# Convolution taps of a state-space stage: shifted copies made through a DRAM scratch in place of copies inside SBUF

## The chip, the cores and the metric

The kernel is one program on one core of a Trainium2 chip. The metric is the device time of that program in microseconds (us), median of several executions. TensorE is PE in the rows of the profile (its weight loads PEld), VectorE is DVE, ScalarE is ACT, GpSimd is POOL. SyncE (SP, its DMA queue SPq) computes nothing here: it waits on semaphores and issues DMAs.

## The reference

Two transformer-like layers run on `x` of 32 batches x 128 steps x 128 channels. The change lies in the first layer's second stage, a Mamba-2 block, which begins with a causal depthwise convolution over 16 steps on 384 channels (256 of `x`, 64 of `B`, 64 of `C`):

```python
zxbcdt = x @ W_in
z = zxbcdt[..., :D_INNER]
xBC = zxbcdt[..., D_INNER:D_INNER + CONV_DIM]
dt = jax.nn.softplus(zxbcdt[..., -NHEADS:] + dt_bias)
kernel = conv_w.T[:, None, :]
xBC = jax.lax.conv_general_dilated(xBC, kernel, window_strides=(1,), padding=[(D_CONV - 1, 0)], ...,
                                   feature_group_count=CONV_DIM) + conv_b
xBC = jax.nn.silu(xBC)
```

A scan over the 128 steps, a gated norm and two projections follow. Before this stage stands a GRU over time, behind it an attention block (cond2), a mixture of experts, and then the second layer.

## The kernel before, in words

Each engine has its own instruction stream, written out by Python generators: `weave` takes one turn of each lane in rotation, so the order on an engine is fixed when the program is built, and semaphores alone decide when an instruction starts. In the stage of the change PE, ACT and DVE each weave four lanes: the convolution (`conv_*`), the step sizes (`mdt_*`), and two workers of the scan (`mamba_*`, worker 0 and worker 1), which start some turns later. SP has only the convolution's lane (`conv_sp`), after its loads and before the loads of the next stage.

The convolution is done in 24 pieces. Piece `n` is one group of 128 channels (`n % 3`) for one unit of four batches (`n // 3`), so its tile is 128 partitions x 512. Its steps:

- **In-projection.** PE makes it into PSUM bank 6 (`inputs` in `conv_pe`; `B<-G,win`), two pieces ahead of the taps. ACT copies it into `XP[n % 4]`, a tile of 4 batches x 144 steps of which the first 16 are zero (`inputs` in `conv_act`, semaphore `conv.x`; shown in the trace as `work<-B`, and `spare<-B` for every fourth piece, since `XP[3]` lies in the area `spare`).
- **Shifted copies.** Twelve of the sixteen taps are done on PE as matmuls that contract over 128 partitions = 32 channels x 4 shifts. For that, `XR[n % 2]` (in `spare`, 130 steps for each of 16 rows) holds in partitions 32g to 32g+31 the tile shifted by 3g steps, and along the free axis the four groups `j` of 32 channels. `conv_sp` fills it by 16 DMAs (4 shifts x 4 channel groups) of 32 partitions x 4 batches x 130 words, 65 KB each, when `conv.x` of the piece and the taps of piece n-2 (which used the same buffer) are done.
- **Taps on PE.** In three turns, `m` = 0, 1, 2, each with four matmuls for the four channel groups (`B<-spare,work` in the trace, two records for each matmul, so x8 for one turn and x24 for a piece). They wait for the semaphore `conv.r0` or `conv.r1` of the 16 DMAs, and for `conv.b` of the piece before, which frees the only PSUM bank of the taps (bank 7).
- **The rest.** ACT takes the bank out with the bias (`work<-B,cb`, `conv.b`), DVE adds the last four taps from `XP` (`conv.acc`), ACT makes a tanh, DVE the silu (`conv.silu`).

ACT's order matters here. In the turns of piece n it does the bias of n-1, the tanh of n-2, and then the copy `XP` of piece n+2. After the first piece it also computes the step sizes (`mdt`) and the decays of both workers (`catt<-tri,catt`, eight for each worker and batch), which PE's cumulative sums (`catt,low`) wait for.

Of the kernel before, what the change touches and what calls it, by code (L numbers as in the profile page):

```python
# [6 lines left out]
F32 = mybir.dt.float32  # L7
# [9 lines left out]
class Signals:  # L17
# [15 lines left out]
    def inc(self, name, *key, by=1):  # L33

        self.value[name] = self.value.get(name, 0) + by
        if self.counting:
            self.place[(name, *key)] = self.value[name]
        return self.sem(name), by

    def dma(self, name, *key):  # L40
        return self.inc(name, *key, by=16)

    def at(self, name, *key):

        if self.counting:
            return self.sem(name), 1
        return self.sem(name), self.place[(name, *key)]
# [54 lines left out]
def act(e, out, in_, func, bias=0.0, scale=1.0):  # L102
    return e.activation(out, in_, func, bias=bias, scale=scale)  # L103
# [35 lines left out]
NT = 12  # L139
# [24 lines left out]
class Kernel:  # L164
# [26 lines left out]
    def sb(self, name, shape, dt=F32):  # L191
        return self.ctx.enter_context(self.nc.sbuf_tensor(name, shape, dt))
# [399 lines left out]
    def lay_mamba(self):  # L592
        sb = self.sb
        self.win = sb("win", [128, 648])
        self.wout = sb("wout", [128, 2, 128])
        self.wnl = sb("wnl", [128, 128])
        self.bnl = sb("bnl", [128, 1])
        self.nw = sb("nw", [128, 2])
        self.cw = sb("cw", [128, 3, 16])
        self.cb = sb("cb", [128, 3])  # L600
        self.dtb = sb("dtb", [128, 8])
        self.alog = sb("alog", [128, 8])
        self.dcol = sb("dcol", [128, 2])
        self.dg = sb("dg", [128, 2, 128])
        self.h0 = sb("h0", [128, 2, 64])
        self.h0T = sb("h0T", [64, 256])
        self.cwp = sb("cwp", [128, 12, NT // 4])
        self.id32 = sb("id32", [128, 32])
        self.tap = self.area([self.work, 74 * 256 - 96 * NT], [128, 3 * NT, 32])
        w = [self.spare, 0]  # L610
        self.XR = [self.area(w, [128, 16, 127 + NT // 4]) for _ in range(2)]
        w = [self.work, 0]
        ar = lambda *s, dt=F32: self.area(w, list(s), dt)
        self.cvb = [ar(128, 3, 512) for _ in range(4)]
        self.c0b = [ar(128, 512) for _ in range(3)]
        self.XP = [ar(128, 4, 144) for _ in range(3)]
        self.XP.append(self.area([self.spare, 5120 - 576], [128, 4, 144]))
        self.cth = [ar(128, 512) for _ in range(2)]
        c = [self.catt, 6144]
        self.adt, self.dth, self.ec, self.q1, self.q2, self.q3 = (self.area(c, [128, NB, 8]) for _ in range(6))  # L620
        self.mw = []
        for wk in range(2):
            wc = [self.catt, wk * 3072]
            m = {"E": [self.area(wc, [128, 8, 128]) for _ in range(2)], "z": [self.area(wc, [128, 256]) for _ in range(2)]}
            m |= {"xdt": ar(128, 256), "cbm": ar(128, 128), "y4": ar(128, 4, 256), "sq": self.area(c, [128, 256]),
                  "ss": ar(128, 4), "yT": ar(128, 2, 512), "tm": ar(128, 512)}
            self.mw.append(m)
# [172 lines left out]
    def conv_act(self, e):  # L800

        at, inc = self.at, self.inc
        BI, BT = self.bank[6], self.bank[7]

        def taps_out(n):
            u, c = n // 3, n % 3
            e.wait_ge(*at("conv.taps", n))
            if u >= 4 and c == 0:
                e.wait_ge(*at(f"mw{u % 2}.pe", "y", (u - 4) // 2 * 4 + 3))
            act(e, self.cvb[u % 4][:, c, :], BT[:], ACT.Identity, bias=self.cb[:, c:c + 1]).then_inc(*inc("conv.b", n))  # L810

        def tanh(n):
            e.wait_ge(*at("conv.acc", n))
            if n >= 2:
                e.wait_ge(*at("conv.silu", n - 2))
            act(e, self.cth[n % 2], self.cvb[n // 3 % 4][:, n % 3, :], ACT.Tanh, scale=0.5).then_inc(*inc("conv.th", n))
        e.wait_ge(*at("conv.pad"))

        def inputs(n):
            e.wait_ge(*at("conv.in", n))  # L820
            if n >= 4:
                e.wait_ge(*at("conv.acc", n - 4))
                e.wait_ge(*at(f"conv.r{n % 2}", n - 4))
            act(e, self.XP[n % 4][:, :, 16:144], BI[:].rearrange("p (b t) -> p b t", b=4), ACT.Copy).then_inc(
                *inc("conv.x", n))
        inputs(0)
        yield
        inputs(1)
        yield
        n = 0  # L830
        for u in range(8):
            for c in range(3):
                if n:
                    taps_out(n - 1)
                if n >= 2:
                    tanh(n - 2)
                yield
                if n < 22:
                    inputs(n + 2)
                for _ in range(3):  # L840
                    yield
                n += 1
            yield
        taps_out(n - 1)
        tanh(n - 2)
        for _ in range(4):
            yield
        tanh(n - 1)
# [37 lines left out]

    def conv_sp(self, e):

        for n in range(24):
            e.wait_ge(*self.at("conv.x", n))  # L890
            if n >= 2:
                e.wait_ge(*self.at("conv.taps", n - 2))
            else:
                e.wait_ge(*self.at("conv.pad"))
            for g in range(4):
                for j in range(4):
                    e.dma_start(self.XR[n % 2][32 * g:32 * g + 32, 4 * j:4 * j + 4, :],  # L897
                                self.XP[n % 4][32 * j:32 * j + 32, :, 1 + NT // 4 * g:128 + NT // 4 * (g + 1)]).then_inc(*self.dma(f"conv.r{n % 2}", n))

    def conv_pool(self, e):  # L900
        e.wait_ge(*self.at("xt", 7))
# [1799 lines left out]
```

## Time and profile before

| | |
|---|---|
| Median of 3 runs | 2227.7 us (2224.23 to 2228.19) |
| The profiled execution's own time | 2227.43 us |
| Its span in the profile | 2225.7 us |
| PE busy, of the span | 1960.3 us (88%) |
| DVE busy | 1593.2 us (72%) |
| ACT busy | 1006.9 us (45%) |
| DMA issues of the convolution | 384 (288 `spare<-work`, 96 `spare<-spare`) of 65.0 KB |
| The stage of the change | from 234 us to about 600 us of the span |

The span is the time from the first to the last instruction that the profiler shows; the execution's own time is 1.7 us longer. Times in rows are counted from the span's start. A row of the timeline gives start and duration, the instruction, how many are merged into it, and in brackets how long the engine had been idle and what ended that. The taps of piece n begin on PE at 249.27 (n = 0), 259.83, 270.84, 280.53, 290.87, 302.21 (n = 5), and so on up to 546.23 (n = 23).

### The profile page before, as it was taken

The numbers are of one execution on the slowest core, as the hardware profiler recorded it, in microseconds if no ns is written. First come the engines' busy times: TensorE is split into PE (matmuls) and PEld (weight loads), VectorE is DVE, ScalarE is ACT, GpSimd is POOL, SyncE is SP. The second block draws the span as 40 slices with busy tenths as digits, with TensorE's granted clock in tenths as the row PEclk, the third lists the DMA queues.
The fourth block names the chain that finished last, engine by engine and source line by source line (L and its number), as shares of the span: only waits on it lengthen the run. The fifth ranks groups of instructions, "written<-read, shape, count | busy, mean of one in ns | idle before, by whom it ended". The sixth has DMA issues, their size and how long they took to land.

```text
span 2225.7 us, 63875 instructions
## 1 busy us (share of the span) xinstructions
PE 1960.3 (88%) x26197; PEld 1227.9 (55%) x26273; DVE 1593.2 (72%) x3661; ACT 1006.9 (45%) x2843; POOL 466.7 (21%) x816
## 2 busy tenths in 40 slices
PE   8989688888778989887899999967999789999998
PEld 5555233333353434434577767655666456677776
DVE  3444557777647787876988888726989578888887
ACT  3333347666622222122555555433554445555554
POOL 2221000000002343434012122254331111112100
PEclk9999789999969899997999999978999999999999
DMA  3000344332000000002211111016552211111111
GB/s 66 4 4 4 74 99 87 71 85 53 30 24 0 1 1 1 1 1 62 76 45 43 45 43 45 25 38 127 110 100 54 67 40 45 45 45 45 42 57 37
DMA packets 133228, 102.42 MB, mean 46 GB/s; under 512 B 23532, under 2 KB 114244, under 8 KB 131364
## 3 DMA queue, kind: packets, MB, share of 16 engines
q1 hardware_dynamic: 129352, 96.04, 17.8%
q8 instruction: 206, 3.38, 0.6%
q10 hardware_dynamic: 3584, 2.30, 0.3%
q14 instruction: 86, 0.70, 0.1%
HBM read 60.24 MB, written 11.82 MB: 32 GB/s over the span
## 4 chain that ended last, share of the span: by engine, by line
PE 47%; DVE 24%; ACT 12%; issue 9%; SPq 3%; DMA 2%; ACTq 1%; POOL 1%; another core or an unknown queue 0%; DVEq 0%; POOLq 0%
PE B L85 46%; DVE work L2251 4%; ACT catt L103 4%; DVE work L107 4%; DVE hr L2215 3%; DVE work L2259 3%; SPq L897 2%; ACT hr L103 2%; ACT ltc L103 2%; ACT work L103 2%; DVE work L1627 1%; DVE gzh L107 1%; ACT ghh L103 1%; ACTq L2538 1%; DVE lth L107 1%
## 5 line engine op out<-in xcount | busy, mean ns | idle before, releaser
L85 PE MATMUL B<-gr,wres 128*128 128x512 f32 x1248 | 352.9, 411 | 15.8 <-DVE work L2259 9.4
L103 ACT ACTIVATE work<-B 128x512 f32<-128x512 f32 (+6 forms) x462 | 236.3, 528 | 143.8 <-PE B L85 99.4
L2301 POOL COPY G<-lh 128x32 f32<-128x32 f32 x256 | 148.3, 579 | 679.9 <-DVE lh L107 679.9
L85 PEld LDWEIGHTS B<-gr,wres 128*128 128x128 f32 x1248 | 214.1, 189 | 82.6 <-DVE work L2259 26.8
L103 ACT ACTIVATE hr<-work 128x512 fp32r<-128x512 f32 x272 | 172.9, 636 | 147.8 <-DVE work L2259 77.8
L2215 DVE TENSOR_TENSOR hr<-work,hr 128x512 fp32r<-128x512 f32 x272 | 186.5, 686 | 8.1 <-ACT hr L103 6.6
L2251 DVE TENSOR_TENSOR work<-work 128x512 f32<-128x512 f32 x256 | 178.6, 698 | 14.7 <-ACT work L103 7.2
L85 PE MATMUL B<-hr,wres 128*128 128x512 f32 x624 | 178.0, 394 | 1.0 <-DVE hr L2215 1.0
L103 ACT ACTIVATE lth<-B 128x96 f32<-128x96 f32 (+1 forms) x512 | 86.7, 222 | 185.9 <-PE B L85 185.8
L85 PEld LDWEIGHTS B<-lh,lw 128*32 128x32 f32 x8128 | 88.5, 112 | 112.8 <-issue 58.6
L85 PE MATMUL B<-lh,lw 128*32 128x32 f32 x8128 | 116.7, 199 | 25.1 <-DVE lh L107 24.3
L107 DVE SCALAR_TENSOR_TENSOR work<-B,ckc,work 128x512 f32<-128x512 f32 x160 | 116.6, 741 | 27.6 <-ACT work L103 18.3
L85 PE MATMUL B<-work 128*128 128x128 bf16 (+2 forms) x1120 | 122.7, 232 | 15.5 <-DMA work<-work 6.2
L85 PEld LDWEIGHTS B<-hr,wres 128*128 128x128 f32 x624 | 117.2, 188 | 28.0 <-DVE hr L2215 1.9
L1627 DVE TENSOR_TENSOR work<-B,work 128x512 f32<-128x512 f32 x160 | 106.6, 680 | 34.9 <-remote 33.9
L103 ACT ACTIVATE catt<-catt 128x512 f32<-128x512 f32 (+2 forms) x142 | 81.7, 590 | 109.3 <-DVE catt L2551 89.8
L1664 POOL TENSOR_TENSOR work<-work 128x512 f32<-128x512 f32 x64 | 82.1, 1283 | 212.5 <-DVE work L1627 118.5
L107 DVE SCALAR_TENSOR_TENSOR lh<-lth,ltc 128x32 f32<-128x32 f32 x256 | 49.4, 193 | 106.3 <-ACT ltc L103 106.3
L85 PE MATMUL B<-gr,hr 128*128 128x512 f32 x384 | 114.1, 435 | 9.5 <-DVE gr L1566 7.0
L85 PE MATMUL B<-X,lw 128*128 128x128 f32 x512 | 121.5, 322 | 0.0
L85 PEld LDWEIGHTS B<-work 128*128 128x128 bf16 (+2 forms) x1120 | 86.0, 108 | 63.4 <-issue 26.7
L85 PE MATMUL B<-gr,wr 128*128 128x512 f32 x384 | 109.6, 420 | 4.0 <-DVE work L2259 2.2
(270 smaller groups left out, 3850.2 us busy)
## 6 DMA issues: line engine op xcount, KB each, us to landing
work<-wdr SPq DMA_DIRECT2D x128, 256.0 KB, 3.1
spare<-work SPq DMA_DIRECT2D x288, 65.0 KB
scr<-catt SPq DMA_DIRECT2D x144, 64.0 KB, 2.8
spare<-spare SPq DMA_DIRECT2D x96, 65.0 KB
work<-scr SPq DMA_DIRECT2D x16, 384.0 KB
work<-scr SPq DMA_DIRECT2D x16, 192.0 KB
catt<-in_L_ffn_ew SPq DMA_DIRECT2D x24, 128.0 KB, 2.4
work<-scr SPq DMA_DIRECT2D x16, 128.0 KB
```

What stands on the lines that cost most here:

```text
L85: return e.matmul(out, lhsT, rhs, start=start, stop=stop, skip_group_check=True)
L103: return e.activation(out, in_, func, bias=bias, scale=scale)
L107: return e.scalar_tensor_tensor(out=out, in0=a, scalar=s, in1=b, op0=op0, op1=op1)
L897: e.dma_start(self.XR[n % 2][32 * g:32 * g + 32, 4 * j:4 * j + 4, :], self.XP[n % 4][32 * j:32 * j + 32, :, 1 + NT // 4 * g:128 + NT // 4 ...
L1627: e.tensor_tensor(four(pr[n % 6]), four(B[:]), KP[:, c, :, j:j + 128], ALU.mult).then_inc(*inc(dve, "v", i, c, j))
L1664: e.tensor_tensor(av, u0, u1, ALU.add).then_inc(*inc(f"cd{wk}.pool", i, c))
L2215: e.tensor_tensor(hr[1][:], self.hh[j % 4], hr[0][:].bitcast(F32), ALU.subtract).then_inc(*self.inc("m.dve", "h", li, j))
L2251: e.tensor_tensor(src, self.sg[i], self.Wb[n % 4], ALU.mult).then_inc(*inc("m.dve", "pu", li, k))
L2259: h = stt(e, self.hh[m], U, 0.5, src, ALU.mult, ALU.mult) if li else e.tensor_tensor(self.hh[m], U, src, ALU.mult)
L2301: e.tensor_copy(self.G[:, :, t], self.lh[:, t % 4, :]).then_inc(*inc("l.pool", "h", li, t))
L2538: e.dma_start(self.aQ[u % 4][48 + q:49 + q, :, :], self.anT[16 * q:16 * q + 16, :]).then_inc(*self.dma("at.max", u))
```

## The change

Each piece now goes out to a scratch in DRAM (`xdr`, four buffers of 32 x 16 x 144 words) by one DMA of 288 KB, and comes back by four DMAs, one for each shift `g`, of 32 partitions x 16 rows x 130 words (260 KB). The transposition of the channel groups (128 partitions x 4 batches into 32 partitions x 16) is done by the outgoing DMA's address pattern on the DRAM side. The outgoing DMA of piece n+1 is issued ahead of the four incoming ones of piece n. Two new semaphores, `conv.w0` and `conv.w1`, count the outgoing DMAs; ACT's copy into `XP` of piece n waits for the outgoing DMA of n-4 in place of the 16 copies of n-4. Everything else of the program is the same.

```diff
         self.XR = [self.area(w, [128, 16, 127 + NT // 4]) for _ in range(2)]
+        self.xdr = [self.nc.dram_tensor(f"xdr{i}", [32, 16, 144], F32, kind="Internal").ap() for i in range(4)]
...
-                e.wait_ge(*at(f"conv.r{n % 2}", n - 4))
+                e.wait_ge(*at(f"conv.w{n % 2}", n - 4))
...
     def conv_sp(self, e):
 
+        at, dma = self.at, self.dma
+
+        def write(n):
+            e.wait_ge(*at("conv.x", n))
+            if n >= 4:
+                e.wait_ge(*at(f"conv.r{n % 2}", n - 4))
+            e.dma_start(self.xdr[n % 4].rearrange("p (j b) t -> j p (b t)", j=4), self.XP[n % 4][:]).then_inc(
+                *dma(f"conv.w{n % 2}", n))
+        e.wait_ge(*at("conv.pad"))
+        write(0)
         for n in range(24):
-            e.wait_ge(*self.at("conv.x", n))
+            if n < 23:
+                write(n + 1)
+            e.wait_ge(*at(f"conv.w{n % 2}", n))
             if n >= 2:
-                e.wait_ge(*self.at("conv.taps", n - 2))
-            else:
-                e.wait_ge(*self.at("conv.pad"))
+                e.wait_ge(*at("conv.taps", n - 2))
             for g in range(4):
-                for j in range(4):
-                    e.dma_start(self.XR[n % 2][32 * g:32 * g + 32, 4 * j:4 * j + 4, :],
-                                self.XP[n % 4][32 * j:32 * j + 32, :, 1 + NT // 4 * g:128 + NT // 4 * (g + 1)]).then_inc(*self.dma(f"conv.r{n % 2}", n))
+                e.dma_start(self.XR[n % 2][32 * g:32 * g + 32, :, :],
+                            self.xdr[n % 4][:, :, 1 + NT // 4 * g:128 + NT // 4 * (g + 1)]).then_inc(*dma(f"conv.r{n % 2}", n))
```

Only SP's stream changes its order. This is SP at the start of the convolution before the change, pieces 1 to 3 (`spare` on the left is `XR`, on the right `XP`):

```order
L897 DMA spare<-work 32x4x130 [waits s_conv.pad,s_conv.x]
L897 DMA spare<-work 32x4x130 x15
L897 DMA spare<-work 32x4x130 [waits s_conv.taps,s_conv.x]
L897 DMA spare<-work 32x4x130 x15
L897 DMA spare<-spare 32x4x130 [waits s_conv.taps,s_conv.x]
L897 DMA spare<-spare 32x4x130 x15
```

And this is SP at the same place with the change, up to the first incoming DMA of piece 3 (`xdr0` to `xdr3` are the four scratches, in DRAM):

```order
L896 DMA xdr0<-work 4x32x576 [waits s_conv.x,s_conv.pad]
L896 DMA xdr1<-work 4x32x576 [waits s_conv.x]
L907 DMA spare<-xdr0 32x16x130 [waits s_conv.w0]
L907 DMA spare<-xdr0 32x16x130 x3
L896 DMA xdr2<-work 4x32x576 [waits s_conv.x]
L907 DMA spare<-xdr1 32x16x130 [waits s_conv.w1]
L907 DMA spare<-xdr1 32x16x130 x3
L896 DMA xdr3<-spare 4x32x576 [waits s_conv.x]
L907 DMA spare<-xdr2 32x16x130 [waits s_conv.taps,s_conv.w0]
L907 DMA spare<-xdr2 32x16x130 x3
L896 DMA xdr0<-work 4x32x576 [waits s_conv.r0,s_conv.x]
L907 DMA spare<-xdr3 32x16x130 [waits s_conv.taps,s_conv.w1]
```

Sixteen DMAs per piece have become five, the shape of the outgoing one begins with 4 where all the others begin with 32, and ahead of the incoming DMAs of a piece there now stands a wait for `conv.x` of the next piece.

## Rows read from the trace of the kernel before

**Rows 1.** View of waits, 228 to 600 us: who waited for whom, total us, times, longest.

```profile
PE B L85 <- DMA spare<-work: 19.1, 5, 7.0
PE B L85 <- DMA spare<-spare: 5.1, 1, 5.1
```

**Rows 2.** Stretch, us, busy of PE, PEld, DVE, ACT, POOL; PE's clock, DMA share, GB/s.

```profile
236.00:302.00 66.00, 41.85 (x203) 12.77 (x200) 33.47 (x82) 21.55 (x52) 0.00 (x0) 0.72 0.45 98
```

**Rows 3.** Timeline of SP's queue: the convolution's first 48 DMA issues.

```profile
236.01 32.44 SPq L897 DMA_DIRECT2D spare<-work  x48
```

**Rows 4.** The DMA issues of the convolution: duration of one, min/median/max ns.

```profile
L897 SPq DMA_DIRECT2D spare<-work x288: 585/601/2046, 236.0 to 524.1; - x144
```

**Rows 5.** Timeline of PE: the taps (spare,work) and the first sums (catt,low).

```profile
249.27 5.24 PE L85 MATMUL B<-spare,work 128*32 128x512 f32 x24 [7.05 <-DMA spare<-work]
259.83 1.93 PE L85 MATMUL B<-spare,work 128*32 128x512 f32 x8 [4.11 <-DMA spare<-work]
261.70 5.08 PE L85 MATMUL B<-catt,low 128*128 128x512 f32 x8
266.70 1.94 PE L85 MATMUL B<-spare,work 128*32 128x512 f32 x16
270.84 1.93 PE L85 MATMUL B<-spare,work 128*32 128x512 f32 x16 [0.29 <-ACT work L103]
280.53 4.97 PE L85 MATMUL B<-spare,work 128*32 128x512 f32 x24 [5.07 <-DMA spare<-spare]
290.87 3.64 PE L85 MATMUL B<-spare,work 128*32 128x512 f32 x16 [4.32 <-DMA spare<-work]
302.21 1.94 PE L85 MATMUL B<-spare,work 128*32 128x512 f32 x8 [2.82 <-DMA spare<-work]
...
324.43 1.07 PE L85 MATMUL B<-spare,work 128*32 128x512 f32 x8
335.15 1.07 PE L85 MATMUL B<-spare,work 128*32 128x512 f32 x8 [0.82 <-DMA spare<-work]
...
363.46 1.07 PE L85 MATMUL B<-spare,work 128*32 128x512 f32 x8
```

**Rows 6.** Timeline of ACT: decays, and copies into XP (pieces 0,1,3-6,8,11).

```profile
235.38 0.60 ACT L103 ACTIVATE work<-B 128x512 f32<-128x512 f32 x1 [2.20 <-PE B L85]
239.50 0.60 ACT L103 ACTIVATE work<-B 128x512 f32<-128x512 f32 x1 [1.03 <-PE B L85]
256.14 4.77 ACT L103 ACTIVATE catt<-tri,catt 128x128 f32<-128x128 f32 x16
260.81 0.57 ACT L103 ACTIVATE spare<-B 128x512 f32<-128x512 f32 x1
271.81 0.59 ACT L103 ACTIVATE work<-B 128x512 f32<-128x512 f32 x1
276.95 0.58 ACT L103 ACTIVATE work<-B 128x512 f32<-128x512 f32 x1
286.68 0.59 ACT L103 ACTIVATE work<-B 128x512 f32<-128x512 f32 x1
313.89 0.60 ACT L103 ACTIVATE work<-B 128x512 f32<-128x512 f32 x1
...
352.07 0.59 ACT L103 ACTIVATE spare<-B 128x512 f32<-128x512 f32 x1
```

**Rows 7.** DMA, 235.9 to 240.9 us: busy tenths in slices of 0.125 us.

```profile
DMA  0000000000004982627840178510000000497303
```

**Rows 8.** DMA, 256.8 to 260 us: packets of the copies inside SBUF.

```profile
DMA packets 720, 0.33 MB, mean 104 GB/s; under 512 B 80, under 2 KB 720, under 8 KB 720
```

**Rows 9.** DMA, 9 to 13 us: loads of 512 B runs from DRAM, all engines busy.

```profile
DMA packets 2510, 1.18 MB, mean 296 GB/s; under 512 B 216, under 2 KB 2510, under 8 KB 2510
```

**Rows 10.** DMA, 608 to 612.5 us: loads, nearly half of the packets of 4 KB.

```profile
DMA packets 831, 1.69 MB, mean 376 GB/s; under 512 B 35, under 2 KB 476, under 8 KB 830
```

**Rows 11.** DMA, 1045.8 to 1047.2 us: one DMA out to DRAM, 8 rows of 2 KB.

```profile
DMA packets 16, 0.02 MB, mean 12 GB/s; under 512 B 8, under 2 KB 8, under 8 KB 16
```

## The prediction

> **What bounds the kernel now.** I read three views, in this order. The view of waits over the stage says what PE waits for: 24.2 us of its idle time end when a copy into `XR` lands, six waits in all [rows 1]. The stretches say where: from 236 to 302 us PE is busy for 41.9 of 66.0 us, at a clock of 0.72, with DVE and ACT busy for 33.5 and 21.6 us, so that no engine is the bound there, and neither are the DMA engines at a share of 0.45 [rows 2]. The timeline of SP then shows what is: 48 issues without a gap take 32.44 us, 0.676 us each [rows 3, 4], or 10.8 us for the 16 of a piece, and the taps of pieces 1 to 5 start 10.6, 11.0, 9.7, 10.3 and 11.3 us after each other [rows 5]. The waits of PE in it are 7.05, 4.11, 5.07, 4.32 and 2.82 us. From piece 6 on both workers of the scan fill PE, and only 0.82 us more is lost, before piece 8 [rows 5]. So all that the change can win lies between 249 and 335 us, and is at most about 24 us.
>
> **What the change does, part by part.** *Issues.* Five for 16 at 0.6 us each [rows 4], some 3.2 us of SP per piece: SP is no bound any more. *What is late next* is the latency from ACT's copy to a filled `XR`, because it now has two DMAs in series, and because SP issues the incoming four of piece n only behind the outgoing one of piece n+1. They cannot start before ACT has made the copy of piece n+1. I call R the time from the end of that copy to the moment when PE can use `XR` of piece n.
>
> R has four terms. (a) From issue to first packets: the first issue is at 236.01 and the busy tenths begin in the 13th slice, at 237.4, so 1.4 us [rows 3, 7]. (b) The outgoing 295 KB. A DMA with 8 outermost rows of 2 KB shows 8 small packets beside 8 large ones [rows 11], while the five issues with 32 outermost partitions show 80, so 16 each [rows 8]. I take the small packets as one closing packet for each DMA engine used: a leading 8 ran on 8 engines, and the outgoing DMA leads with 4. Large packets run at 376 GB/s over 16 engines [rows 10], 23.5 per engine, so four engines need 295/94 = 3.1 us, where 16 would need 0.8. (c) The incoming DMAs are queued behind it on these four engines. Each engine has 128 packets of 520 B and 4 small ones. A packet takes 25.5 ns in the loads (4 us x 16 / 2510) [rows 9] and about 34 ns in the copies into 32 partitions (0.45 x 16 x 460 B / 98 GB/s, with 0.33 MB / 720 = 460 B) [rows 2, 8]: 3.4 to 4.5 us. I take the middle, 3.9. (d) Landing: the 32nd issue, the last of piece 1, ended near 236.01 + 32 x 0.676 = 257.6 and began 0.6 before; PE went on at 259.83, 2.8 us after its begin. Less 1.4 for (a) and 0.6 of packets (five slices), 0.8 us are left [rows 3, 5, 7]. R = 1.4 + 3.1 + 3.9 + 0.8 = 9.2 us. The 0.65 us of the outgoing issue and 2.6 us of the four incoming ones lie beside (b).
>
> By the Trainium skill (DMA: Bandwidth & Descriptors, Rules for kernel authors) "an outermost dim of size c < 16" confines a whole DMA to at most c engines; the 8 closing packets agree with it, and it speaks against this change, whose outgoing pattern puts the four channel groups outermost. By this rule (b) is 3.1 us, as taken; without it, 0.8.
>
> *The walk.* Pieces 0 and 1 first. The copies of 0 and 1 end at 235.98 and 240.10 [rows 6]. Outgoing 0 has landed at 236.0 + 1.4 + 3.1 + 0.8 = 241.3. Outgoing 1 holds its four engines until 244.6, incoming 0 follows on them until 248.5: PE can start at 249.3, as before (249.27). On these engines outgoing 2 takes until 251.6 and incoming 1 until 255.5, so `XR` of piece 1 is ready at 256.3. PE comes to it at 259.83 - 4.11 = 255.7, and starts 3.5 us earlier than before. Next come the sums of both workers. They need the decays, which ACT ends at 258.5 (first eight) and 260.9 [rows 6] and which do not move. The first worker's sums run from 258.5, the second's end at 260.9 + 2.5 = 263.4, where both ended at 266.78. So the rest of the taps of piece 1 is 3.1 us earlier.
>
> From here each piece has two bounds, and the later one counts: PE's arrival (its start before, less its wait, less the lead won so far), and the copy of the next piece + R.
> - Piece 2: copy 3 ends at 261.4 and stands behind the decays, so it does not move; + 9.2 = 270.6, against 270.84. Lead 0.2.
> - Piece 3: copy 4 ended at 272.4, and follows the taps of piece 1, so 269.3 + 9.2 = 278.5, against 280.53. Lead 2.0.
> - Piece 4: copy 5, 277.53 - 0.2 = 277.3, gives 286.5; PE arrives at 286.55 - 2.0 = 284.5. Against 290.87, lead 4.4.
> - Piece 5: copy 6, 287.27 - 2.0 = 285.3, gives 294.5; PE arrives at 299.39 - 4.4 = 295.0. Against 302.21, lead 7.2.
> - Piece 8: the last 0.8 us of waiting. Lead 8.0. The starts of all of these are in [rows 5, 6].
>
> In the later pieces the distance from a copy to the taps of the piece before it must be over 9.2 us. The smallest is 324.43 - 314.49 = 9.9, the next is 363.46 - 352.66 = 10.8 [rows 5, 6]; of the rest one more has 10.8 and six have 11.1 to 11.9. So there R is hidden, if with little to spare. What covers the double latency is the scan's work on PE.
>
> *At no cost:* ACT's copy waits for the outgoing DMA of n-4 in place of the copies of n-4, both long done; the wait of an outgoing DMA for the incoming ones of n-4 likewise; the 33 MB through DRAM meet no other transfer of the stage. Behind the wait for the copy of n+1 SP has only the incoming DMAs of n, counted in R. After the convolution SP's next loads wait for the scan's end. A shorter wait could also raise PE's clock from 0.72 [rows 2]; I book nothing for it.
>
> The sum is made against the profiled execution's own 2227.4 us, 0.3 below the median of the runs: 2227.4 - 8.0 = 2219.4 us.
>
> **Bounds.** The unknown prices are (b) and (c). With (b) at 3.1 and (c) at 3.4 and landing half a microsecond shorter, R = 8.2, and the same walk gives a lead of 11 us. With R = 10 it gives 6.5. If the outgoing packets take half as long again (4.6 us), R = 10.7, and 4 us are left. Reads of DRAM into 32 partitions are not in the trace; their two neighbours are the ends of (c).
>
> The copies inside SBUF run at 98/0.45 = 218 GB/s of all engines, the loads into 128 partitions at 296 [rows 2, 9]. By the Trainium skill (SBUF — State Buffer, Door 1: The DMA port swizzle) 32 partitions reach 8 of 16 ports and end near 218 GB/s; the trace agrees. By this the incoming DMAs would take 4.9 us where all engines run together, R would be about 10, and the time 2221.
>
> **The rivals.**
> 1. *The outgoing DMA runs on 16 engines.* Then (b) is 0.8, R = 6.9, piece 0 starts 2.3 us earlier, the walk gives leads of 4.8, 6.6, 10.9 and 13.7 us at pieces 2 to 5 and 14.5 in the end: 2213 us. For it: the source leads with 128 partitions, and the transfer is large. Against it: the 8 closing packets [rows 11].
> 2. *R is 10.2 to 11.5*, since outgoing packets into DRAM are slow, or the issue of the incoming ones stalls behind the four busy engines (single issues took up to 2.05 us [rows 4]). The waits then stay on the early pieces, with another cause: a lead of 6 down to 0, at R = 10.9 some 3.5 us: 2224 us.
> 3. *Slower.* With R = 12 the copy of the next piece decides everywhere, in the full part of the stage too. The walk then gives leads of -2.6, -0.8, -1.2 and +1.6 us at pieces 2 to 5. Piece 7 loses 2.1 us (12 against 9.9), the two with 10.8 lose 1.2 each, and the six others 0.1 to 0.9 each, 3.1 together: 7.6 lost, 1.6 + 0.8 won, so 2233 us. It decides from R = 11.5 on. For it: two DMAs in series on four engines, and a wait of SP for the piece after. Against it: it needs 2.8 us more than rows show anywhere.
>
> **How the numbers follow.** The forecast (lead 6 to 11 us) has 0.52, rival 1 (over 11) 0.16, rival 2 (lead under 6) 0.22, rival 3 0.10. The likeliest gives 2219.4 us. The range reaches down to 2212, which takes in rival 1 at its price, and up to 2225.5, which takes in nearly all of rival 2. A measurement of this kernel can tell 0.2%, 4.5 us, from no change. Forecast and rival 1 are all faster by more, and a third of rival 2: 0.75. The rest of rival 2 and a little of rival 3 lie within: 0.17. Slower: 0.08.
>
> **What the profile would show.** The outgoing DMAs should show four small packets each, and bursts on a quarter of the engines. PE's first taps should start within a microsecond of 249.3, its later waits for the incoming DMAs should be near 0.6, 2.9, 3.3 and 2.0 us at pieces 1 to 4, none at 5, and 9 us should lie between the end of ACT's copy of a piece and the taps of the piece before it, at pieces 2 to 4. From piece 6 on the timeline should be the old one, 7 to 8 us earlier, and so the rest of the kernel. I am wrong if PE's first taps start near 247 (16 engines), if waits on DMA appear at pieces 7 and 10 (R over 10), or if the lead won by 302 us is given back before 600.

## The result, and the profile after

The changed kernel takes 2238.2 us, the median of 20 runs, against 2225.5 us of as many runs of the kernel before: a ratio of 1.0060, with a 95% interval of 1.0048 to 1.0072. It is about 13 us slower, where 2219.4 was forecast and 2225.5 was the upper end of the range. That is a change of 0.6%, small but clear of the noise. Rival 3 of the prediction came true in kind (2233 us, chance 0.10). The profiled execution took 2237.95 us, its span 2236.2; before they were 2227.43 and 2225.7. So 10.5 of the 13 us are to be found in the two traces.

PE's waits from 228 to 610 us, us in total, times, the longest:

```profile
PE B L85 <- DMA spare<-xdr: 35.7, 12, 11.2
```

It was 24.2 us in six waits [rows 1]. SP issues little now and sleeps long: the wait ahead of the outgoing DMA (L896) holds it for 180 us, half of the stage. The view of SP's waits, from 228 to 600 us:

```profile
SPq L896 <- ACT work L103: 124.0, 15, 14.4
SPq L896 <- ACT spare L103: 56.3, 6, 11.2
```

The taps of PE (start, duration, then in brackets PE's wait before them), for pieces 0 to 4 and then where a wait on `XR` is left:

```profile
253.49 4.83 PE L85 MATMUL B<-spare,work 128*32 128x512 f32 x24 [11.19 <-DMA spare<-xdr]
260.19 1.07 PE L85 MATMUL B<-spare,work 128*32 128x512 f32 x8 [0.65 <-DMA spare<-xdr]
...
277.23 3.64 PE L85 MATMUL B<-spare,work 128*32 128x512 f32 x16 [6.68 <-DMA spare<-xdr]
284.80 2.79 PE L85 MATMUL B<-spare,work 128*32 128x512 f32 x24 [0.99 <-DMA spare<-xdr]
296.78 3.64 PE L85 MATMUL B<-spare,work 128*32 128x512 f32 x16 [8.14 <-DMA spare<-xdr]
...
317.89 1.08 PE L85 MATMUL B<-spare,work 128*32 128x512 f32 x8 [0.25 <-DMA spare<-xdr]
328.22 1.07 PE L85 MATMUL B<-spare,work 128*32 128x512 f32 x8 [1.08 <-DMA spare<-xdr]
337.96 1.07 PE L85 MATMUL B<-spare,work 128*32 128x512 f32 x8
...
370.09 1.07 PE L85 MATMUL B<-spare,work 128*32 128x512 f32 x8 [1.15 <-DMA spare<-xdr]
412.76 1.07 PE L85 MATMUL B<-spare,work 128*32 128x512 f32 x8 [1.22 <-DMA spare<-xdr]
...
549.12 1.07 PE L85 MATMUL B<-spare,work 128*32 128x512 f32 x8 [2.04 <-DMA spare<-xdr]
```

Against [rows 5], pieces 0 to 4 start 4.2, 0.4, 6.4, 4.3 and 5.9 us later, and piece 8 (337.96) 2.8 us later. Before, PE waited for `XR` nowhere after piece 8. Now it does at pieces 10, 13, 16, 19 and 22.

R can be read off against the copies of ACT (pieces 3, 4 and 5):

```profile
264.63 0.57 ACT L103 ACTIVATE spare<-B 128x512 f32<-128x512 f32 x1
272.32 0.58 ACT L103 ACTIVATE work<-B 128x512 f32<-128x512 f32 x1
283.93 0.59 ACT L103 ACTIVATE work<-B 128x512 f32<-128x512 f32 x1
```

The copy of piece 3 ends at 265.20 and PE starts on piece 2 at 277.23: R = 12.0. The next two give 284.80 - 272.90 = 11.9 and 296.78 - 284.52 = 12.3; at pieces 6, 7, 10, 13, 16 and 19 it is 11.7 to 12.1. It was taken as 9.2. It is longer at piece 22 (12.9), and at pieces 0 and 1 (13.3 and 17.3), whose outgoing DMAs queue behind others. SP's queue, which [rows 3] showed as 48 issues in a row, is now:

```profile
236.11 4.61 SPq L896 DMA_DIRECT2D xdr<-work  x2
242.85 2.69 SPq L907 DMA_DIRECT2D spare<-xdr  x4
...
265.23 0.56 SPq L896 DMA_DIRECT2D xdr<-spare  x1
266.30 3.54 SPq L907 DMA_DIRECT2D spare<-xdr  x4
```

Outgoing 0 is issued at 236.11, and the first incoming DMA, which waits for it, at 242.85: 6.7 us for 295 KB (the 288 KB above in units of 1024 bytes). From 237.3 to 242.3 us it runs all but alone (slices of 0.125 us):

```profile
DMA  1243904900200013221331112222222222242119
GB/s 55 55 55 37 150 0 18 37 0 0 18 0 0 18 55 74 74 74 55 74 55 55 74 55 111 111 92 111 92 111 111 92 111 92 111 111 74 55 55 74
```

It begins well, then hardly a packet starts for a microsecond (single packets of 2304 B take up to 1.0 us, against 0.09 in the median), then it goes at 55 to 74 GB/s, and only in its last part at 92 to 111. These are 23 to 28 GB/s for each of four engines, the rate that was taken for the whole. Over its packets, some 5.2 us, it moves 57 GB/s, 14 from each. What makes the start slow was not tried. In e2 below, where the same DMA stands behind incoming ones on its engines, it has no such start, and its packets take 3.3 to 3.9 us at pieces 1 to 8, nearer to the 3.1 of the prediction.

That it is four engines is shown by the small packets from 228 to 600 us:

```profile
DMA packets 53891, 33.13 MB, mean 89 GB/s; under 512 B 1632, under 2 KB 50784, under 8 KB 53856
```

1632 = 96 x 16 for the incoming DMAs + 24 x 4 for the outgoing ones. The rule of the Trainium skill that the prediction weighed (DMA: Bandwidth & Descriptors, Rules for kernel authors: an outermost size below 16 bounds the number of engines) agrees.

*R, taken apart.* The trace also holds the time at which each engine reports its share of a DMA to the semaphore. Outgoing 3, issued at 265.23, is reported by its four engines at 271.12, 271.26, 272.71 and 272.79. The last report of the incoming DMAs of piece 2 comes at 277.19, and PE starts at 277.23. So 7.6 us pass until the outgoing DMA has landed, and 4.4 more until the incoming ones have. At the other pieces of early and full part at which PE waits (3, 4, 6, 7, 10, 13, 16, 19) the two parts are 7.6 to 8.7 and 3.3 to 4.6 us, in the median 7.7 and 4.0. The view of the DMA engines from 266 to 278 us (slices of 0.3 us) shows why the second part is short:

```profile
DMA  0150527696677989999999997432239997366997
```

From 267.7 the other twelve engines already carry their shares of the incoming DMAs, and by 273.8 they are done. From there to 275 only the four late engines still work, at 0.2 to 0.3 of 16.

The incoming issues (duration of one, min/median/max ns) became longer too:

```profile
L907 SPq DMA_DIRECT2D spare<-xdr x96: 538/984/2073, 242.9 to 546.8; - x96
```

An incoming issue takes 0.98 us in the median, where issues had taken 0.60 [rows 4]. This is not in the chain: the last of piece 2 ends at 269.83, before the outgoing DMA has landed at 272.79, and it is so at every early piece.

*Where the 10.5 us arise.* The last taps start at 568.92, before at 553.86: 15.1 us later. Of these 2.8 were there at piece 8, and 12.3 come in the full part, in which six pieces take 89.0 us in place of 85.3. The stretches (columns as in [rows 2]), first of before, then of after:

```profile
345.00:430.30 85.30, 74.14 (x826) 32.59 (x826) 62.52 (x109) 58.12 (x141) 3.55 (x2) 0.98 0.36 78
```

```profile
349.00:438.00 89.00, 75.66 (x828) 32.55 (x824) 62.64 (x109) 58.09 (x140) 3.54 (x2) 0.96 0.42 93
```

Of the 3.7 us, two waits of 1.15 and 1.22 us are idle time, and 1.5 us is busy time of PE for the same work at a clock of 0.96 in place of 0.98. Over the whole full part (335.15 to 553.86 before, 337.96 to 568.92 after) PE is busy for 195.5 us in place of 190.7, so 4.8 of the 12.3 us are busy time, and 6.7 are waits for `XR`. About 4 us are given back later, in the stage after the scan, of before and of after:

```profile
660.10:1032.30 372.20, 324.19 (x1363) 151.66 (x1376) 287.83 (x475) 81.14 (x132) 146.31 (x118) 0.93 0.01 2
```

```profile
674.60:1042.50 367.90, 322.67 (x1382) 148.93 (x1376) 287.71 (x475) 81.11 (x132) 146.28 (x118) 0.94 0.01 2
```

The first stretch begins 14.5 us later and the end lies 10.2 later. PE's busy time accounts for 1.5 of the 4.3 us; the rest is idle time, whose cause was not tried.

### The profile page after: what moved, and what is told of

It is laid out like the page before. It is cut to its first block, busy times and chain, and to the rows that moved or that the text cites. A ratio compares the mean times of both kernels' runs of the same rounds, so it can differ in the third digit from the quotient of the medians.

```text
span 2236.2 us, 63706 instructions
## 1 busy us (share of the span) xinstructions
PE 1966.7 (88%) x26273; PEld 1225.0 (55%) x26273; DVE 1593.4 (71%) x3661; ACT 1006.7 (45%) x2843; POOL 466.0 (21%) x816
## 4 chain that ended last, share of the span: by engine, by line
PE 46%; DVE 24%; ACT 12%; issue 8%; DMA 5%; SPq 2%; ACTq 1%; POOL 1%; DVEq 0%; POOLq 0%
PE B L85 44%; DVE work L2261 5%; DVE work L107 4%; DMA spare<-xdr 3%; ACT catt L103 3%; DVE hr L2225 3%; DVE work L2269 3%; ACT hr L103 2%; ACT work L103 2%; ACT ltc L103 2%; ACTq L2548 1%; DVE gzh L107 1%; ACT ghh L103 1%; SPq L907 1%; DVE work L1637 1%
## 5 line engine op out<-in xcount | busy, mean ns | idle before, releaser
L85 PE MATMUL B<-gr,wres 128*128 128x512 f32 x1248 | 354.5, 412 | 16.5 <-DVE work L2269 10.2
L107 DVE SCALAR_TENSOR_TENSOR work<-B,ckc,work 128x512 f32<-128x512 f32 x160 | 116.6, 741 | 27.0 <-ACT work L103 17.6
L85 PE MATMUL B<-spare,work 128*32 128x512 f32 x576 | 81.8, 657 | 35.7 <-DMA spare<-xdr 35.7
```

The costliest lines, as they stand in the source:

```text
L85: return e.matmul(out, lhsT, rhs, start=start, stop=stop, skip_group_check=True)
L107: return e.scalar_tensor_tensor(out=out, in0=a, scalar=s, in1=b, op0=op0, op1=op1)
```

## The experiments

Two theories of why R is 12: (A) the outgoing DMA holds four engines for long, and the incoming packets and issues queue behind it; (B) the order is to blame, since the incoming DMAs of a piece are issued only behind the outgoing one of the next. Both can be true, and each has its own cure. A third theory, (C) in the texts below, was that the incoming DMAs are slow by themselves. All edits are against the changed kernel except where said. In the table the second number is the kernel before on the same chip, and the ratio is to it, with its 95% interval; the last column is PE's time waiting for `XR` and the number of waits.

| run | time, us | before, us | ratio | waits |
|---|---|---|---|---|
| before | | 2225.5 | | 24.2, 6 |
| the change | 2238.2 | 2225.5 | 1.0060 (1.0048 to 1.0072) | 35.7, 12 |
| e1_out16 | 2219.8 | 2225.4 | 0.9970 (0.9954 to 0.9986) | 21.7, 6 |
| e2_order | 2225.8 | 2225.4 | 1.0000 (0.9986 to 1.0013) | 25.0, 6 |
| e3_both | 2216.8 | 2225.4 | 0.9964 (0.9949 to 0.9979) | 16.2, 5 |
| e4_twice | 2278.1 | 2225.4 | 1.0240 (1.0222 to 1.0257) | 60.4, 14 |
| e5_long_in | 2216.7 | 2224.2 | 0.9964 (0.9950 to 0.9977) | 17.3, 4 |
| e6_both_long | 2209.3 | 2224.2 | 0.9931 (0.9916 to 0.9946) | 12.2, 5 |
| e7_direct_long | 2224.3 | 2224.2 | 1.0008 (0.9995 to 1.0020) | 21.5, 5 |
| e8_in128 | 2200.3 | 2225.2 | 0.9885 (0.9841 to 0.9929) | 9.7, 4 |
| e9_in32 | 2212.6 | 2225.2 | 0.9952 (0.9920 to 0.9984) | 17.6, 5 |
| e10_one_in_before | 2214.8 | 2226.5 | 0.9947 (0.9926 to 0.9968) | 13.7, 4 |
| e11_one_in_behind | 2206.4 | 2226.5 | 0.9904 (0.9876 to 0.9932) | 5.2, 4 |

**e1_out16**: the outgoing copy in four DMAs of 32 partitions each, which run on 16 engines; the order stays.

```diff
-            e.dma_start(self.xdr[n % 4].rearrange("p (j b) t -> j p (b t)", j=4), self.XP[n % 4][:])...
+            for j in range(4):
+                e.dma_start(self.xdr[n % 4][:, 4 * j:4 * j + 4, :], self.XP[n % 4][32 * j:32 * j + 32])...
```

> The outgoing transfer of a piece is four DMAs of 32 partitions (each leads with 32, so 16 engines) in place of one that leads with 4. Nothing else changes. R is the time from the end of ACT's copy of piece n+1 to the first taps of piece n where PE waits for them; it was 11.7 to 12.3 us in the changed kernel. Theory A (four engines carry the outgoing bytes, and incoming packets and their issues are queued behind them): incoming issues fall from a median of 984 ns to about 600, R falls to 8.5 to 9.5 although SP issues three more DMAs (1.9 us), no wait for the incoming DMAs after piece 6, and the time is 5 to 10 us below that of the kernel before. Theory C (the incoming DMAs of 512 runs out of DRAM are slow by themselves): issues stay near 1 us, R stays at 12 or grows by the 1.9 us to 13 to 14, and the time is 12 to 25 us above before.

```profile
263.46 1.71 SPq L897 DMA_DIRECT2D xdr<-spare  x4
265.27 2.55 SPq L908 DMA_DIRECT2D spare<-xdr  x4
...
273.31 3.64 PE L85 MATMUL B<-spare,work 128*32 128x512 f32 x16 [4.53 <-DMA spare<-xdr]
```

R is 273.31 - 263.43 = 9.9 us, 2.1 less than with four engines, if more than the 8.5 to 9.5 expected; the incoming issues are back at 0.627 us in the median, and of the waits at pieces 10 to 22 only 0.33 us is left. This edit alone turns 13 us slower into 6 us faster, so (A) is shown. Outgoing copy 3 lands 3.0 us after its first issue in place of 7.6, yet R falls by 2.1 only. From the first incoming issue to PE it still takes 8.0 us, and the packets of 520 B in it take 5.9: R is not the 6.9 of rival 1. So (C) holds in part as well, if not in the 12 to 25 us that it forecast: once all 16 engines bring the incoming bytes together, they take longer than the four late engines of the changed kernel took for their own shares.

**e2_order**: the outgoing DMA stays on four engines, and `write(n + 1)` stands behind the incoming issues of piece n.

```diff
-            if n < 23:
-                write(n + 1)
             e.wait_ge(*at(f"conv.w{n % 2}", n))
 ...
             for g in range(4):
                 e.dma_start(self.XR[n % 2][32 * g:32 * g + 32, :, :], ...
+            if n < 23:
+                write(n + 1)
```

> The outgoing DMA stays on its four engines, but SP issues the incoming DMAs of piece n before the outgoing one of piece n+1, so they no longer wait for ACT's copy of n+1. Theory B (the place in SP's order is what makes the latency count in the full part of the stage): the five or six waits of about 1.1 us each from piece 6 on are gone, PE's first taps start 2 to 3 us earlier than in the changed kernel (near 250.5), a piece of the early part costs SP one landing of the outgoing DMA (6.7 us) and the four issues (2.6 us), 9.3 to 10.5 in all, so the time is 3 to 8 us below before. If the order does not matter (the latency is the engines' work itself), it stays within 4 us of the changed kernel, 12 us above before.

```profile
274.71 2.57 SPq L905 DMA_DIRECT2D spare<-xdr  x4
277.38 0.55 SPq L896 DMA_DIRECT2D xdr<-work  x1
285.07 2.56 SPq L905 DMA_DIRECT2D spare<-xdr  x4
287.73 0.55 SPq L896 DMA_DIRECT2D xdr<-work  x1
295.55 2.56 SPq L905 DMA_DIRECT2D spare<-xdr  x4
```

Now there is no wait behind piece 8 (0.54 us), since in the full part a copy lies long ahead of its use. In the early part each piece costs SP a whole round: 2.6 us of incoming issues, then 7.7 us until the outgoing DMA has landed behind them, 10.4 us per piece. That is the pace of the kernel before (9.7 to 11.3 us [rows 5]), and so is the time. (B) holds too, 12 us against the change, but as an exchange: in the full part it wins what the change lost, in the early part it puts the outgoing DMA's landing into the chain. The 3 to 8 us below before that were expected did not come.

**e3_both**: both edits.

> Both edits: four outgoing DMAs of 32 partitions, issued behind the incoming ones of the piece before. Under A and B together the outgoing transfer lands 5 us after its first issue, the incoming ones after 5 to 6 more, PE's waits in pieces 1 to 5 fall to under 10 us in total, none later: 8 to 14 us below before. Under C it equals the order edit alone or is 2 to 4 us slower than it.

The round falls from 10.4 to 9 us (incoming issues at 269.70, 278.68, 287.31), and the time to 9 us below before. From the first incoming issue to PE: 277.89 - 269.70 = 8.2 and 286.63 - 278.68 = 8.0 us. The packets of 520 B of piece 3 last from 271.04 to 276.92, so 5.9 us, with 1.3 us before and 1.0 behind. The engines from 269 to 279 us (slices of 0.25 us):

```profile
DMA  0000000078899999999999999999999996200000
```

The outgoing packets, issued at 273.38, come behind on the same engines, the first at 276.16. So this is what an incoming copy takes when nothing is ahead of it: 1.07 MB in 5.9 us, 181 GB/s. PE's waits, 16.2 us, are more than the 10 expected; the time is at the near end of its range.

**e4_twice**: the suspected cost doubled. The outgoing DMA is issued twice, on its four engines, the first time into a second scratch that nobody reads.

```diff
+            for dst in (self.xdd, self.xdr):
+                e.dma_start(dst[n % 4].rearrange("p (j b) t -> j p (b t)", j=4), self.XP[n % 4][:])...
```

> The outgoing DMA is issued twice, the first time to a scratch that nobody reads; both lead with 4. Theory A: four engines get 3.1 us (at their full rate) or more of extra work ahead of the incoming packets, R grows from 12 to 15 to 16 us, waits for the incoming DMAs appear at nearly all pieces, and the time is 45 to 65 us above before. Theory C: R grows only by the extra issue, 0.6 us, and the time is 15 to 25 us above before.

52.7 us slower than before, so 40 us slower than the change, as (A) had it. R is 14.6 to 15.7 us at pieces 2 to 4. The incoming issues behind it stretch further:

```profile
L909 SPq DMA_DIRECT2D spare<-xdr x96: 539/1124/4122, 247.8 to 581.8; - x96
```

**e5_long_in** and **e6_both_long**: what the short packets of 520 B cost. `XR` rows are made 144 words wide, so that each of the 32 partitions gets one run of 9160 B in place of 16 short ones (the fourth `XP` moves to make room). e5 is e1 with it, e6 is e3 with it.

```diff
-        self.XR = [self.area(w, [128, 16, 127 + NT // 4]) for _ in range(2)]
+        self.XR = [self.area(w, [128, 16, 144]) for _ in range(2)]
 ...
+                s = 1 + NT // 4 * g
+                e.dma_start(flat2(self.XR[n % 2])[32 * g:32 * g + 32, 0:2290],
+                            flat2(self.xdr[n % 4])[:, s:s + 2290])...
```

> As the run with four outgoing DMAs, and the rows of XR are 144 words wide, so that an incoming DMA is 32 runs of 9160 B (2290 words) in place of 512 runs of 520 B; 10% more bytes. From the first incoming issue to PE's go the runs so far showed 7.9 to 8.4 us, where 1.4 + 0.8 us and the prediction's 3.9 us would be 6.1. Theory P (short packets are what makes the incoming part long, 44 ns each on 132 per engine): with 1.17 MB at the 376 GB/s of large packets it takes 3.1 + 2.2 + about 0.5 = 5 to 6 us, R falls from 9.9 to 7 to 8, and the time is 10 to 14 us below before. Theory Q (32 partitions as the target set the pace, near 200 GB/s): 5.5 to 6 us of transfer, no shorter than with short runs, R stays at 9.5 to 10.5 and the time at 5 to 9 us below before.

> As the run before, with the outgoing DMAs issued behind the incoming ones of the piece before. Theory P: outgoing 4.6 us + incoming 5.5 = 10 us per piece from ACT's copy of the same piece, PE's waits under 12 us in total, 10 to 15 us below before. Theory Q: as with short runs, 6 to 10 us below before.

From the first incoming issue to PE it is 7.2 to 7.5 us in e5 (281.21 to 288.74 for the latter) and 7.2 to 7.7 in e6, some 0.6 us less. The packets of an incoming copy, now 1.17 MB, take 5.7 us in the median of e5 and 5.8 of e6 (5.5 at the shortest, with no other transfer beside them), 206 GB/s where short packets had 181. So short packets do cost, about an eighth of the rate, but the long rows carry 10% more bytes, and little is won: the 3.1 us of theory P are far away. R in e5 is 9.0 to 9.4. e6 is 14.9 us below before, where e3 is 8.6, and this lies in the range of theory P, though its packets do not. Of the 4.0 us less waiting in its trace 3.2 are at piece 0, where the first outgoing copy landed after 3.1 us in place of 4.6; nothing in the edit accounts for that. Why e6 gains as much is open.

**e7_direct_long**: the kernel before, with the 16 transfers inside SBUF flattened to 32 runs of 562 words each.

> The kernel before with the same 16 DMAs inside SBUF per piece and no scratch, but rows of 144 words in XR, so that each DMA has the shape 32 x 562 words in place of 32 x 4 x 130. If an issue takes the 0.42 us that the outgoing DMAs of shape 32 x 576 take, and not the 0.60 of the three-dimensional ones, a piece takes SP 16 x 0.46 = 7.4 us in place of 10.8, and PE's waits of 24 us shrink to 6 to 12: 10 to 17 us below before. If the issue time does not hang on the shape, nothing changes (within 3 us).

```profile
L901 SPq DMA_DIRECT2D spare<-work x384: 507/591/1957, 236.0 to 538.8; - x192
```

No difference: 0.591 us in place of 0.601 [rows 4], and the time is that of before. The expectation that a flat shape shortens the issue from SBUF to SBUF fell; the short issues of 0.42 us were seen only where one side is in DRAM. The old kernel's bound could not be eased in this way.

**e8_in128** and **e9_in32**: what the 32 target partitions cost. In both, the incoming DMAs read as many bytes from the input `x` in place of the scratch, so the convolution works on other data: in e8 into all 128 partitions, 573 words each, in e9 into 32 partitions, 2292 words each. The rest is e6.

```diff
+                x = self.I["x"].rearrange("b (q t) d -> (b q) (t d)", q=4)
 e8: +                e.dma_start(flat2(self.XR[n % 2])[:, 573 * g:573 * g + 573], x[:, 573 * g:573 * g + 573])...
 e9: +                e.dma_start(flat2(self.XR[n % 2])[32 * g:32 * g + 32, 0:2292], x[32 * g:32 * g + 32, 0:2292])...
```

> A measurement of the incoming part, on the kernel with both edits and long rows. The four incoming DMAs of a piece take their words from the input x in DRAM (so the convolution works on other data), each into all 128 partitions, 573 words of each; its twin takes the same bytes from the same place by four DMAs of 32 partitions and 2292 words. If the number of target partitions sets the pace, this one needs 1.17 MB / 376 GB/s = 3.1 us where the twin needs 5.2, and the time from the first incoming issue to the taps that wait for it is 5.3 to 6.3 us here and 7.2 to 7.7 in the twin. If it does not, both show 7.2 to 7.7. The whole kernel: 2 to 4 us faster than the twin, or the same.

> The twin: four incoming DMAs of 32 partitions x 2292 words each out of the input x (the convolution works on other data). From the first incoming issue to the taps that wait for it 7.2 to 7.7 us, as in the kernel with both edits and long rows; a shorter time here would mean that reading back what was just written is what costs.

```profile
271.00 1.77 SPq L910 DMA_DIRECT2D spare<-in_x  x4
...
276.83 1.93 PE L85 MATMUL B<-spare,work 128*32 128x512 f32 x16 [2.08 <-DMA spare<-in_x]
```

```profile
268.03 1.71 SPq L910 DMA_DIRECT2D spare<-in_x  x4
...
275.64 4.28 PE L85 MATMUL B<-spare,work 128*32 128x512 f32 x24 [2.66 <-DMA spare<-in_x]
```

5.8 us against 7.6, for the same bytes from the same tensor in as many DMAs, with runs that are four times shorter in the faster one. The number of target partitions sets the pace. Reading back what was just written costs nothing that shows: e9, which reads the input, takes 7.6 us, no less than e6. e8 is 12 us faster than its twin, where 2 to 4 were expected; with two runs of e8 and five of e9 this size is uncertain, and the finding rests on the traces.

**e10_one_in_before** and **e11_one_in_behind**: can the real kernel have 128 targets? Partition 4r + g holds channel r, shifted by g, in place of partition 32g + r, with the rows of the filter and of the summing matrix permuted to match. Then a single DMA fills `XR`, so the number of incoming DMAs changes too, from four to one; e8 and e9 differ in the partitions alone. e10 has the order of the change, e11 that of e2; both have the outgoing copy of e1 and the long rows.

```diff
-            pairs.append((self.cwp[32 * g:32 * g + 32, :, :], taps[...]))
+            pairs.append((self.cwp[g:128:4, :, :], taps[...]))
 ...
-        red(e, self.id32[:], self.ident[:].rearrange("p (j m) -> p m j", j=4), ALU.add)...
+        red(e, self.id32[:], self.ident[:].rearrange("p (m j) -> p m j", j=4), ALU.add)...
 ...
+            x = self.xdr[n % 4]
+            e.dma_start(flat2(self.XR[n % 2])[:, 0:2290],
+                        bass.AP(tensor=x.tensor, offset=x.offset + 1, ap=[[2304, 32], [NT // 4, 4], [1, 2290]]))...
```

> One incoming DMA into all 128 partitions of XR (partition 4r+g in place of 32g+r, with the filter's rows and the summing matrix permuted to match), outgoing DMAs on 16 engines, long runs, in the order of the change (outgoing n+1 ahead of incoming n). Theory (the 32 target partitions set the pace of the incoming transfer, and nothing else of the chain is at stake): from the incoming issue to PE 6 us, as in the run with 128 partitions, R = 1.8 + 6 = 7.8 us against 9.4 with 32-partition targets, no wait of PE on it after the first pieces, four waits of about 12 us in all, and a time 11 to 16 us below the kernel before. Rival (the pace of the incoming transfer comes from the overlapping reads of DRAM, which the run on the input did not have): from issue to PE 7.5 us as with 32 partitions, and 6 to 9 us below the kernel before.

> The same, with the outgoing DMA of piece n+1 issued behind the incoming one of piece n. Theory: outgoing 4.6 us, incoming 6 us, PE waits 8 to 11 us in all, all on pieces 1 to 5, and a time 20 to 27 us below the kernel before, as the run that took other data into 128 partitions (25 below). Rival (overlapping reads of DRAM set the pace): incoming 7.5 us, waits of 12 us, and 15 us below, as with the long runs into 32 partitions.

```profile
268.46 0.52 SPq L909 DMA_DIRECT2D spare<-xdr  x1
...
274.54 3.62 PE L85 MATMUL B<-spare,work 128*32 128x512 f32 x16 [2.30 <-DMA spare<-xdr]
```

From issue to PE it takes 6.1 us here and 5.4 to 5.6 in e10 (270.35 to 275.86). The transfer into 128 and into 32 partitions, both in long runs, is best seen in slices: e11 from 268 to 275 us (slices of 0.175 us), then e6 from 272 to 280.5 (0.2125 us); the incoming packets begin in the 11th and the 7th slice, and in both the 295 KB of the next outgoing copy follow at the end.

```profile
DMA  0000000000991799989999899644866999631000
GB/s 13 0 0 0 0 0 0 0 0 0 523 262 52 314 419 419 471 366 471 419 419 419 314 262 419 157 105 157 314 262 263 382 369 395 224 119 40 26 26 0
```

```profile
DMA  0000009429992992899588998894679589641000
GB/s 0 0 0 0 0 0 517 129 86 388 431 302 43 345 302 43 172 259 216 129 216 259 216 259 216 172 388 86 140 140 227 141 271 347 228 174 65 0 0 0
```

The engines are as busy in both, but move 314 to 471 GB/s in the one and mostly 129 to 302 in the other. The 128 packets of 9160 B of the incoming copy last 4.4 us (269.76 to 274.15) in the one and 5.8 (273.28 to 279.11) in the other; the medians are 3.9 us for e10 and e11, and 5.8 for e6. The rival, that overlapping reads of DRAM set the pace, fell: e10 and e11 overlap as e6 does. e10 is 12 us below before with R = 7.3 us (268.08 - 260.80), with somewhat more waiting than expected (13.7 us against about 12). e11 waits less than was expected, 5.2 us against 8 to 11, and is 20 us below before, at the short end of its 20 to 27. Of the versions that do the whole computation it is the best: 2206.4 us against 2226.5 of before and 2238.2 of the change. Its interval still touches that of e6, and the two did not run beside each other.

## Why the prediction was wrong

- *The bound of the kernel before, and that issues cease to be it:* right. SP waits for 180 us of the stage now.
- *R decides, at the copy of the next piece:* right. Nine of PE's twelve waits end 11.7 to 12.3 us after ACT's copy of the next piece (13.3, 17.3 and 12.9 at pieces 0, 1 and 22).
- *(b), the outgoing packets on four engines, taken as 3.1 us:* this is the step that failed. From issue to the last report the outgoing DMA takes 7.7 us in the median; less 1.4 for (a) and 0.8 for (d), 5.5 us are left for (b), or 4.5 for outgoing 0 by itself. The number of engines was right. The rate of each came from loads that went the other way, on all engines at once [rows 10], and held only in the last part of each transfer. Of the 2.8 us by which R was short, (b) has some 2.4. The prediction priced 4.6 us as a bound, at 4 us of lead, but alone.
- *(c), the incoming packets, taken as 3.9 us:* about right in the changed kernel, 4.0 us in the median between the two landings, but with only four engines left at work, which the prediction did not reckon with (that this makes them faster is an argument, no run tests it alone). Where all 16 bring the incoming bytes together, as in e1 and e3, (c) is 5.9 us, and 1.07 MB in 5.9 us are 181 GB/s, below both rows that it was taken from, the loads into 128 partitions at 296 GB/s [rows 9] and the copies inside SBUF at 218 [rows 2, 8]. So 3.9 was luck, and by this term rival 1's R of 6.9 could not come: from the incoming issue to PE alone e1 has 8.0. The rule of the Trainium skill on ports (SBUF — State Buffer, Door 1: The DMA port swizzle), by which 32 partitions reach half of the ports and end near 218 GB/s, was named in the prediction and not used in its sum. The 206 GB/s of e5 in long runs (215 at its shortest) agree with it, e8 against e9 agrees with its direction, and the 181 GB/s of short packets lie below it.
- *(a) and (d), 1.4 and 0.8 us:* right as a pair. Outgoing 3 has 1.2 us from issue to first packet and 0.5 from last packet to last report, the incoming copy of e3 1.3 and 1.0.
- *The sum:* 1.4 + 5.5 + 4.0 + 0.8 = 11.7 us, where 11.7 to 12.3 are measured. This is past 11.5, from which rival 3 decides.
- *The walk:* rival 3 gave leads of -2.6, -0.8, -1.2 and +1.6 us at pieces 2 to 5; measured are -6.4, -4.3, -5.9 and -3.4. Most of the difference is the 3.8 us by which ACT's copy of piece 3 moved (264.63 against 260.81 [rows 6]). It stands behind the decays, and these behind the taps of piece 0, which started at 253.49. The walk had held the decays fixed because it had piece 0 at 249.3.
- *The distances in the full part:* read wrongly. Before, it is 10.6 and 10.5 us at pieces 13 and 19, and 10.8 at three pieces (10, 16, 22), not two:

```profile
393.18 1.08 ACT L103 ACTIVATE work<-B 128x512 f32<-128x512 f32 x2 [0.81 <-PE B L1004]
404.88 1.07 PE L85 MATMUL B<-spare,work 128*32 128x512 f32 x8
478.49 1.08 ACT L103 ACTIVATE work<-B 128x512 f32<-128x512 f32 x2 [0.81 <-PE B L1004]
490.06 1.07 PE L85 MATMUL B<-spare,work 128*32 128x512 f32 x8
```

The second copy of each pair, which ends at 394.3 and 479.6, is the one that counts. With all distances right rival 3 loses 10.7 us there and not 7.6, and its time is 2236, not 2233. The five pieces and piece 7 are where PE waits: 7.8 us in all, 6.7 of them behind piece 8. That PE's busy time would grow too, by 4.8 us of the 12.3, no term had.
- *The chances:* rival 3 got 0.10, with "it needs 2.8 us more than rows show anywhere" against it. Each bound was walked by itself. The upper ends together, 1.4 + 4.6 + 4.5 + 0.8 = 11.3, were 0.2 us from where it decides; that alone asked for more than 0.10.

Right were the signs it named for itself: four small packets for each outgoing DMA, and waits at pieces 7 and 10 if R is over 10.

## What to carry to other kernels

When an issue-bound row of small transfers is replaced by two transfers in series, write down the latency of the chain, price each DMA by the number of engines that its outermost size gives it *and* by the number of partitions at its SBUF end, and add the upper bounds together before calling a case unlikely. A DMA on four engines is worse than its own time: whatever is queued behind it waits on those four. Put the bytes on 16 engines and the targets on all 128 partitions (here it took a permutation of the weights, wider rows and one address pattern). Try both places for the next piece's outgoing copy: behind this piece's incoming one it had the lower median in all four pairs of runs here, clear of noise in two (the change against e2, e5 against e6).

## What the runs showed of the hardware

- A DMA of 295 KB from SBUF to DRAM on four engines, in rows of 2304 B, takes 6.7 us from issue to landing when it is alone and 7.7 in the median with incoming DMAs on the other engines, with packets of up to 1.1 us in its first 2 us. Over its packets this is 12 to 14 GB/s for each engine, in its last part 23 to 28. As four DMAs on 16 engines the same bytes land 3.0 to 3.8 us after the first issue in e1 at all but four pieces, 1.7 of it the issues.
- The incoming issues took 0.98 us in the median (up to 2.07) behind one outgoing DMA on four engines, 1.12 (up to 4.12) behind two, 0.63 (up to 1.24) behind four on 16. It is not enough that engines have work ahead: in e2 an outgoing DMA issued right behind four incoming ones took 0.55.
- An issue takes 0.42 us for a flat read of DRAM into 32 partitions or a flat write from 32, 0.52 for a read with three dimensions into 128, 0.62 for rows of 16 runs, and 0.60 and 0.59 from SBUF to SBUF in two shapes.
- The packets of 1.17 MB from DRAM in long runs take, in the median, 5.7 to 5.8 us into 32 partitions per DMA (e5, e6, e9), 4.7 into 128 in four DMAs (e8) and 3.9 in one (e10, e11). In runs of 520 B, 1.07 MB into 32 take 5.9 (e1, e3).
